# A decoder layer on one core: a new order of all engines' jobs in the pair loop

## The reference

```python
x = x + self_attention(layernorm(x))            # one head of 256: a causal softmax, a softmax over
                                                # means of 4 keys, and one over the 64 largest
                                                # scores (the others 0); mean of three, then Wo
x = x + cross_attention(layernorm(x), ctx, ctx, mask)   # 16 heads of 64, additive mask
x = x + ffn(layernorm(x))                       # 256 -> 1024 -> 256, gelu, inputs and weights
                                                # rounded to 127 steps of their largest value
```

## Time and profile before

| | |
|---|---|
| median of 3 runs | 1675.04 us (1672.29 to 1675.15) |
| profiled execution | 1671.48 us, span of its instructions 1669.4 us |
| PE busy | 1573.6 us (94%) |
| DVE busy | 1461.2 us (88%) |
| ACT busy | 1060.9 us (64%) |
| POOL busy | 1051.2 us (63%) |
| granted TensorE clock, mean | 0.983 |

### The profile page before, as it was taken

How to read it: one execution, slowest core, us unless ns; L and a number is a source line. 1 busy time by engine, 2 the same in 40 slices (tenths; PEclk the granted TensorE clock), 3 DMA queues, 4 the chain that set the end, 5 groups by cost and what they waited for, 6 DMA issues and landing times.

```text
span 1669.4 us, 51921 instructions
## 1 busy us (share of the span) xinstructions
PE 1573.6 (94%) x16058; PEld 1401.0 (84%) x16058; DVE 1461.2 (88%) x6184; ACT 1060.9 (64%) x2205; POOL 1051.2 (63%) x1168
## 2 busy tenths in 40 slices
PE   6799999999999999999999999999999999778898
PEld 5689999999999999999999999999999998644465
DVE  4889999999999999999999999999999996679876
ACT  4456666666666666666666666666666666469875
POOL 4557777777777777777777777777777776621000
PEclk9999999999999999999999999999999999789999
DMA  6000000000000000000000000000000000221155
GB/s 211 8 15 29 28 28 28 25 28 28 28 27 22 26 28 28 28 28 28 28 28 28 28 28 22 22 28 28 25 28 28 28 28 17 90 85 51 60 178 166
DMA packets 77732, 71.01 MB, mean 43 GB/s; under 512 B 6272, under 2 KB 77184, under 8 KB 77696
## 3 DMA queue, kind: packets, MB, share of 16 engines
q1 hardware_dynamic: 76736, 70.41, 13.4%
q10 hardware_dynamic: 960, 0.13, 0.1%
HBM read 45.36 MB, written 25.17 MB: 42 GB/s over the span
## 4 chain that ended last, share of the span: by engine, by line
PE 73%; DVE 14%; ACT 6%; issue 4%; POOL 1%; DMA 0%; ACTq 0%; DVEq 0%; SPq 0%; POOLq 0%
PE banks L111 21%; PE banks L112 18%; PE banks L113 18%; PE banks L868 5%; DVE tile_max L2010 4%; PE banks L848 3%; PE banks L892 3%; DVE xn L1241 3%; PE banks L1901 2%; ACT normed L1106 2%; DVE x L1390 1%; DVE ctx_t L1274 1%; ACT ctx_t L1076 1%; DVE kept L2022 1%; PE banks L747 1%
## 5 line engine op out<-in xcount | busy, mean ns | idle before, releaser
L589 POOL TENSOR_TENSOR shifted<-scores,score_max 128x512 f32<-128x512 f32 x256 | 266.9, 1043 | 200.6 <-DVE score_max L1286 159.9
L595 POOL TENSOR_TENSOR exp_t<-exp_copy,exp_t 128x512 f16<-128x512 f32 x256 | 302.5, 1182 | 60.6 <-ACT exp_copy L1091 60.6
L1286 DVE CUSTOM_DVE_ANT_0 scores<-banks,mask 128x128 f32<-128x128 f32 x1024 | 235.0, 286 | 11.6 <-issue 6.0
L1076 ACT ACTIVATE q_t<-banks 128x512 f16<-128x512 f32 x128 | 76.5, 598 | 224.0 <-PE banks L113 224.0
L581 POOL TENSOR_TENSOR v_nat<-kv_copy,v_nat 128x512 f16<-128x512 f32 x124 | 138.8, 1130 | 105.2 <-ACT kv_copy L1079 105.2
L111 PE MATMUL banks<-ctx_t,cross_Wk 128*128 128x256 f32 x512 | 154.7, 302 | 21.8 <-DVE ctx_t L1274 18.5
L1089 ACT ACTIVATE exp_t<-banks 128x512 f16<-128x512 f32 x256 | 155.9, 609 | 6.2 <-PE banks L113 3.8
L1091 ACT ACTIVATE exp_copy<-banks 128x512 f32<-128x512 f32 x256 | 158.6, 620 | 0.0
L868 PE MATMUL banks<-ident,shifted 128*128 128x128 f32 x1024 | 153.8, 279 | 3.9 <-POOL shifted L589 2.8
L111 PE MATMUL banks<-xn_t,cross_Wq 128*128 128x256 f32 x512 | 153.1, 299 | 2.7 <-POOL cross_Wo L269 1.6
L1079 ACT ACTIVATE kv_copy<-banks 128x512 f32<-128x512 f32 x248 | 150.9, 608 | 0.0
(11 more groups left out here) (261 smaller groups left out, 5661.8 us busy)
## 6 DMA issues: line engine op xcount, KB each, us to landing
x_in<-in_x_dram SPq DMA_DIRECT2D x32, 256.0 KB, 2.8
ctx_in<-in_ctx_dram SPq DMA_DIRECT2D x32, 256.0 KB, 2.7
x_residual<-x SPq DMA_DIRECT2D x64, 128.0 KB, 1.7
x_normalised<-normed SPq DMA_DIRECT2D x32, 256.0 KB, 2.1
shared<-x_normalised SPq DMA_DIRECT2D x8, 1024.0 KB, 5.3
shared<-x_residual SPq DMA_DIRECT2D x16, 512.0 KB, 3.8
out_dram<-shared SPq DMA_DIRECT2D x16, 512.0 KB, 2.9
mask<-in_fside_Bx1xSxS_dram SPq DMA_DIRECT2D x64, 64.0 KB, 1.8
```

Source lines behind the costliest of these rows:

```text
L589: pool.tensor_tensor(shifted[:, q % 2], scores[:, q % 2], score_max[:, q % 2, :].unsqueeze(2).to_broadcast([P, QUAD, P]), ALU.subtract).th ...
L595: pool.tensor_tensor(exp_t[:, q % 2, LO], exp_copy[:, q % 2], exp_t[:, q % 2, HI], ALU.subtract).then_inc(exp_split, 1)
L1076: op = act.activation(hilo(dst, *at)[HI], src, ACT.Copy)
L1286: op = dve.tensor_tensor_reduce(scores[:, q % 2, h, :], sc_bank(q)[:, tile(h)], mask[:, b, :], 1.0, NEG, ALU.add, ALU.max, score_max[:, q ...
```

## The change

All five engines get a new list for the body, and the jobs of `fj_bank` new numbers to match. The same operations run, the same number of times. The jobs of the weights' preparation and of the feed-forward's weights, which stand in the lists between the others, come to stand behind other calls. The core of the diff:

```diff
-(J_PT1, J_K0, J_K1, J_PT0, J_AO, J_X, J_K2, J_V0, J_V1, J_G, J_K3, J_X1, J_RAW, J_Q1,
- J_Q0, J_Q2, J_Q3, J_VV0, J_VV1, J_VV2, J_VV3, J_CTX) = range(22)
+(J_PT1, J_K0, J_K1, J_PT0, J_K2, J_X, J_AO, J_V0, J_G, J_V1, J_RAW, J_K3, J_X1, J_Q0,
+ J_Q1, J_Q2, J_Q3, J_VV0, J_VV1, J_VV2, J_VV3, J_CTX) = range(22)
...
             if back:
                 exp_lo(1, i - 1)
+                shift(5, i - 1)
+            if front and not early:
+                lo(J_K0, i)
+            if back:
+                exp_lo(2, i - 1)
             if ahead and not early:
                 reciprocal_deviation(i + 1, moments_x, moments, var_eps, eps_x, rstd, rstd_x)
             if back:
-                exp_lo(2, i - 1)
+                exp_lo(3, i - 1)
                 keep_x1(i - 1)
-                exp_lo(3, i - 1)
-            if front and not early:
-                lo(J_K0, i)
-            if back:
-                shift(5, i - 1)
+                shift(6, i - 1)
+                exp_lo(4, i - 1)
+                shift(7, i - 1)
+                exp_lo(5, i - 1)
             if front and not early:
                 lo(J_K1, i)
...
                 if ahead:
                     lo(J_G, i + 1)
                 if ahead and not front:
                     normalise(1, x_in, moments, rstd, rstd_x, xn, xn_ready)
+                if ahead:
+                    lo(J_V1, i + 1)
+                if front:
+                    normalise(i, x1, moments1, rstd1, rstd_x1, xn1, xn1_ready)
+                if ahead:
+                    raw_scores(i + 1)
```

More of the change, by code:

```diff
@@ L910, in body @@
                 keys(0, i)
+                keys(1, i)
             if back:
[L912 to L914 removed]
+                weigh(1, i - 1)
             if front:
@@ L991, in body @@
                 heads_transpose(3, i - 1)
+            if front and not early:
+                values(1, i)
             if front:
@@ L1129, in body @@
             if back:
-                exponential(4, i - 1)
+                exponential(5, i - 1)
+            if ahead and not early:
+                hi(J_G, i + 1)
             if ahead:
@@ L1136, in body @@
                 weights_of["cross_hi"](act, 12, 16)
-            if ahead and not early:
-                hi(J_G, i + 1)
-            if back:
-                exponential(5, i - 1)
-            if front and not early:
-                hi(J_K3, i)
-            if front:
-                hi(J_X1, i)
             if back:
@@ L1148, in body @@
             if front:
-                hi(J_Q1, i)
+                hi(J_X1, i)
+            if front and not early:
+                hi(J_K3, i)
+            if front:
                 hi(J_Q0, i)
@@ L1158, in body @@
             if front:
+                hi(J_Q1, i)
                 hi(J_Q2, i)
+                hi(J_Q3, i)
+            if front and not early:
+                hi(J_VV0, i)
             if back:
@@ L1453, in body @@
                 if back:
+                    row_sums(0, i - 1)
                     add_mask(5, i - 1)
-                if ahead and front:
-                    statistics(i + 1, x_in, stats, stats_x, moments, moments_x)
-                if back:
-                    row_sums(0, i - 1)
                     divide(0, i - 1)
@@ L1463, in body @@
                     row_sums(1, i - 1)
+                    divide(1, i - 1)
+                if ahead and front:
+                    statistics(i + 1, x_in, stats, stats_x, moments, moments_x)
+                if back:
+                    add_mask(6, i - 1)
                 if front:
                     lo(J_PT0, i)
-                if back:
-                    divide(1, i - 1)
                 if ahead and front:
                     normalise(i + 1, x_in, moments, rstd, rstd_x, xn, xn_ready)
-                if front:
-                    first_residual(i)
                 if back:
-                    row_sums(2, i - 1)
+                    add_mask(7, i - 1)
                     heads_lo(0, i - 1)
@@ L1510, in body @@
                     ffn_of["weight_one"](dve)
-                if ahead:
-                    raw_scores(i + 1)
+                if back:
+                    row_sums(5, i - 1)
                 if ahead and not front:
@@ L1521, in body @@
                 if back:
-                    row_sums(5, i - 1)
+                    divide(5, i - 1)
+                if ahead:
+                    top_round(i + 1, 2)
+                    top_round(i + 1, 3)
+                if ahead and not front:
+                    early_lo(J_G)
+                if front:
+                    lo(J_Q0, i)
+                if ahead:
+                    top_round(i + 1, 4)
+                if back:
+                    row_sums(6, i - 1)
                 if back and not front:
                     ffn_of["quantise"](dve, 0)
-                if ahead:
-                    top_round(i + 1, 2)
                 if front:
```

207 lines of the change are left out of this document (91 added, 116 removed).

## The result

The changed kernel takes 1696.79 us (median of 4 runs, 1695.62 to 1700.0), the kernel before 1673.93 (4 runs on the same chip, 1672.29 to 1675.15): 1.0139 times as long, interval [1.0124, 1.0154]. It is slower by 1.4%, and the forecast of 1695 us lies 1.8 us beside it. The profiled execution took 1697.29 us with a span of 1694.8.

The account below looks back on a forecast made before the run. PE was taken as the bound, DVE just under it. 37.7 + 1.05 + 0.1 + 5.4 less 0.35 gave a 43.9 us period, +0.7 by 30 bodies +20 us: 1691.5 profiled, 1695 median; range 1666 to 1714 us.

Parts of the forecast that it names:

- the front without stops: K0 to the end of out1: 36.94 us before, 37.7 after, with VV2 in, et3 out and K2's wait gone.
- the tail: End of out1 to next K0: 5.4 us, set by DVE's chain to `ctx_t`; PE stands about 1.0 us ahead of K0.
- the tie at out0: At out0: heads low 1 ends at 18.7 us after K0, as out0 wants to start; 0.1 us of stop.
- Fill and drain: Bodies outside the steady loop, run once: put at nothing, 3 us either way.
- The X chain: Row sums, statistics, `rstd`, normalisation of x: X's transposes start at 8.1 instead of 7.05 us after K0, stop 1.05 us.
- The tie: POOL's `exp_lo(3)` at 6.75 against the normalisation's second half at 6.77 us; POOL wins, the half ends at 8.05.
- The X1 chain: Normalisation of x1 meets nothing on POOL: 0.73 us, no stop of PE, 0.3 us to spare.
- DVE as a second bound: DVE's work and new idle times make 43.7 us a period, just under PE, so DVE has no room.
- the first: Second half slips in ahead of `exp_lo(3)`: normalisation ends at 7.2, period 43.1, about 1672 us; chance 0.18.
- The second: First half queues behind `exp_lo(3)`, then `keep_x1`: X at 8.75, period 44.6, 1716 us; chance 0.12.
- The third: PE's blocks between K0 and out1 pack better: period 42.8, 1663 us; chance 0.20.
- the fourth: DVE becomes the bound after out0: with 0.3 us more wait, 1704 us; chance within the forecast's 0.50.

Follow-up runs that it names:

- e4: Changed kernel, loop untouched: three operations moved ahead in the drain (POOL, PE, DVE), DVE's low halves of G and V1 ahead in the fill; 1688.83 us.
- e8: e6 with the three drain edits of e4, without its fill edit; 1655.24 us.
- e10: Changed kernel with the load of the next x and DVE's statistics of x earlier, POOL's order left alone; 1695.32 us.
- e6: Changed kernel with the load of the next x and DVE's statistics earlier, and x's deviation ahead of `exp_lo(2)` on POOL; 1663.88 us.
- e1: Changed kernel with POOL, in the loop, waiting for the normalised x of the next pair ahead of `exp_lo(3)`; 1683.63 us.
- e2: Changed kernel with `add_mask(4)` on DVE back behind `ctx_t`'s low half and the largest of x2; 1779.53 us.
- e3: Changed kernel with the edits of e1 and e2 together; 1730.95 us.
- e7: Changed kernel with DVE's order `ctx_t`'s low half, `add_mask(4)`, then the largest; 1700.85 us.
- e5: e1 with x1's deviation put ahead of K1's low half on POOL; 1673.27 us.
- e12: e8 plus two DVE reorderings in body 0, e7's swap, POOL's x deviation and `exp_lo(2)` before K0's low half, POOL waiting for xn between; 1679.36 us.

## Why the prediction was right, and where it wasn't

The mechanism of the loop held: slower, by a normalisation that meets `exp_lo(3)` and an X stop that it makes. That the time came out within 1.8 us is in part luck. Two errors offset each other: the loop lost 12.8 us where 20 were forecast, the fill and the drain 10.3 where nothing was. And 3.5 us were added for the distance between the profiled execution and the median; by the profiled executions it is 1697.29 against a forecast of 1691.5, a loss of 25.8 instead of 20.

- *The sum for a period.* 43.9 forecast, 43.76 measured. By its terms: the front without stops 37.57 (37.7 forecast), X's stop 0.99 (1.05), the tail 5.20 (5.4). The 0.1 of the tie at out0 didn't come. These four terms were too large by 0.49 together (0.13, 0.06, 0.2 and 0.1). I had taken off 0.35 for small waits in the old front, where only 0.13 is to be found; the rest of it hid the error of the tail. The mean period before is 43.25, not the 43.21 of the window, so the loss in a period was 0.51, not 0.7, and with the shorter first period 12.8 us over the loop instead of 20.
- *Fill and drain.* "I put them at nothing, with 3 us either way" was the term that failed. They cost 4.2 (2.3 with the loop's first period) and 6.15 us; e4 and e8 took 8.6 and 5.8 off their drains with three edits. My ground, the 1 us by which a whole period moves, says nothing about bodies in which half of the jobs are missing: there the waits that the loop covers lie open, 3.3 us for `rstd` in body 31 alone.
- *The X chain.* Its times were right: statistics 4.11 to 5.20 (4.1 to 5.2), `rstd` 6.50 (6.4), normalisation 6.53 to 8.18 (6.45 to 8.05), X at 8.24 (8.1). X itself was due at 7.25, not 7.05, so the stop came out right though X started 0.14 later than forecast. Its cause was wrong by half. I had `rstd` follow from the statistics; the row of POOL says that `exp_lo(2)` ends at 5.39, 0.2 after the moments, and e10 shows that earlier moments alone move nothing. I saw POOL's time (5.3) and put it under a rival.
- *The tie.* It fell as forecast, but not in the forecast's order (6.75 for POOL, 6.77 for the second half): the second half's own row starts at 6.86, POOL's `exp_lo(3)` at 6.88; over 26 periods it lies between 0.01 behind and 0.03 ahead of POOL, and it always ends 0.15 behind POOL. By the order of most of these starts it should have slipped in. My other reason stands: the first half (0.41 long, to 6.94) is still running when POOL starts. In e6 the second half starts 0.28 to 0.31 ahead of `exp_lo(3)` and takes 0.40; where between 0.03 and 0.28 it begins to win, no run shows. e1 shows that this collision is all of the stop.
- *The tail.* The chain from out1 to `ctx_t` on DVE without a pause, and K0 waiting for it with `add_mask(4)` right ahead: both as forecast. The stop is 0.48 by the row, 0.68 with the 0.2 of pipeline that the forecast's 1.0 included, since the chain is 5.20 and not 5.4 long and PE's own work 4.5 and not 4.4. So it did shrink, by about 0.14 against before (0.62 by the row). What I did not see is that this order buys pv1 through POOL's queue (e2, e3, e7).
- *The X1 chain.* 0.74 for the normalisation, 0.96 of DVE's idle ahead of V1's low half (1.2), no stop at X1, as forecast.
- *DVE as a second bound.* Not so. The 43.7 us held 4.75 us of gaps, and 4.5 were measured (43.75 less 39.28); but gaps are waits for others, no load, and they shrink with them: e6 brought the period to 42.67 with the same operations on DVE. What held the next loss was POOL's order (e1, e5), not DVE's load.

The rivals: the condition of the first (the normalisation done by 7.2) is what e1 made at the price of a wait on POOL (done by 7.27, period 43.28, 43.1 forecast) and e6 without one (done by 7.0, period 42.67). The second, the first half behind `exp_lo(3)`, came in e7, where the normalisation runs from 7.27 to 9.11 and X starts at 9.17. The third and the fourth didn't come: X started after 7.4, and no row from out0 to the end of out1 shows PE waiting for DVE.

## What to carry to other kernels

When an engine's rows stand end to end from a late release to the result that is waited for, the queue is the cause, and an input that comes earlier moves nothing by itself (e10): test it by moving the waiting operation in that queue too (e6). A wait that takes away a collision is paid for by whoever stands behind it; look for the next engine that has no pause (e1, e12). Two rows that start within 0.03 us of each other are no ground for saying which will win. And a new order has to be read in the bodies that fill and drain as well: here they carried 8 to 10 of 25 us, and three edits there took 8.6 off the drain.
